# Moving the weight splits of a two-layer FFN kernel's first stage from ScalarE to GpSimd, and reordering VectorE's routing block

## The chip, the cores and the metric

One core of one Trainium2 chip runs the kernel. The metric is the device time of one execution, in microseconds. The engines are TensorE (PE in the rows; PEld is its weight load), VectorE (DVE), ScalarE (ACT), GpSimd (POOL) and SyncE (SP), whose queue issues nearly all the DMAs. Each engine works through its own list of instructions in order, and the engines are tied together by semaphores.

## The reference

x is 128x32x128 (batch, time, channel). Layer 0 is a mixed linear map (a base weight and eight low-rank experts, weighted by cond), then a normalisation, a quantisation of the activations by the maximum over everything, and a ternary weight. Layer 1 routes every batch row to two of eight gated MLPs (128 to 512 and back) and adds a shared one; a quantised gated MLP follows.

```python
def L0_ffn(x, weight, gamma, beta):
    xn = (x - mu) * rsqrt(var + EPS) * gamma + beta      # per row of 128 channels
    xq = round(clip(xn / scale)) * scale                 # scale: max |xn| over all / 127
    return einsum('bsi,oi->bso', xq, ternary(weight))
def mlp(x, g, u, d):
    return einsum(gelu(x @ g) * (x @ u), d)
x = x + L0_ffn(L0_cond(x, cond_8, ...))
y = sum over the row's top-2 experts of w[e] * mlp(x, skill_*[e]) + mlp(x, shared_*)
x = x + L1_ffn(y, w_gate, w_up, w_down)
```

## The kernel before

All products are made in float32r. To keep accuracy, a matrix is split into a high half, which is the matrix copied to float32r, and a low half, the matrix minus the high half; a product is then three matmuls.

**The rounds.** The first stage is a software pipeline of 12 rounds, `n` = 0 to 11, over 8 groups of 512 columns (`i`). Each engine has its own loop over n with the same stages. TensorE transposes x (`turns`), multiplies it with the low-rank matrices (`hidden`) and with the base weight (into the bank `AZ`), sums squares (into `AV`) and spreads the reciprocal deviation over the partitions. ScalarE copies the high half of x (`xTh`), makes the squares (`sq`) and the scaled product (`xnT`), and two rounds later adds beta. VectorE makes the low half (`xTl`), multiplies the hidden part (`hs`), writes variance plus epsilon (`ST`, called ST(i) below, counter `d_var`), multiplies by the reciprocal deviation (`xnT`, xnT(i) below) and takes the maximum. GpSimd raises ST to the power -0.5 (`ST<-ST,KC`, pow(i) below, counter `k_rst`). ST(i) and pow(i) stand in round i + 2; xnT(i) in round i + 3.

**What is slipped in between.** In rounds 2 to 5 VectorE also computes the routing: many operations of 8 to 480 elements on the tiles RT, KS, etC, etF, etA, tmpP and Pm. The last and longest piece stands in round 4 and is called the routing block below.

**The weight splits.** 19 weight tiles are loaded in turn into eight staging buffers `stg`: 16 expert gate and up weights, which are split into a ring of five buffers `wst` and stored to DRAM (`wscr`), and three of the shared MLP, which stay in SBUF. `SPLITS[n]` says how many are split in round n. ScalarE makes the high half (`a_whi`), GpSimd the low half (`k_wlo`). SP waits for low half n, issues its store, then the load that reuses the staging buffer, and from n = 11 on the loads of the down weights (`wdr`). The high halves of the down weights (`down_high`) are made by ScalarE, five of them in rounds 8 to 11, and three later.

**The mixed block.** After the rounds the maximum is found, x is rounded (`round_xn`), multiplied with the ternary weight and added to x, transposed again and split into `XT`, in a second pipeline over `j`; the first eight of the shared MLP's tiles run in it. ScalarE's first copy to XT waits until all 19 low halves are made, since XT lies over stg. GpSimd makes the low halves of the down weights and of the first four shared tiles in turn (`down_low`, `shared_low`), then gathers the columns of the first expert tile (`fetch`, tile `xg`). After that come the expert tiles on TensorE (`xg,Wr`).

Of the kernel before, what the change touches and what calls it, by code (L numbers as in the profile page):

```python
# [16 lines left out]
ADD, SUB, MUL = ALU.add, ALU.subtract, ALU.mult  # L17
# [32 lines left out]
def program(nc, x, cond, Wb, bb, As, Bs, fw, gamma, beta, sg, su, sd, hg, hu, hd, wg, wu, wd, out):  # L50
    ctx = ExitStack()
    with ctx:
# [137 lines left out]
        s_stg = [sem(f"s_stg{i}") for i in range(8)]  # L190
        s_wst = [sem(f"s_wst{i}") for i in range(WRING)]
        s_wr = [sem(f"s_wr{i}") for i in range(3)]
        s_wz, d_ov = sem("s_wz"), sem("d_ov")
# [15 lines left out]
        k_tab, d_tab, p_tab = sem("k_tab"), sem("d_tab"), sem("p_tab")  # L209
        k_wlo, k_rst = sem("k_wlo"), sem("k_rst")  # L210

        d_col, p_max, d_top = sem("d_col"), sem("p_max"), sem("d_top")

# [34 lines left out]
        IOTA, PART, TRI0, IDENT, TRI, CTR, HALVES, MEAN, NONE, PLACES = 3, 4, 5, 6, 7, 8, 9, 10, 11, 12  # L248
        SPLITS = (0, 2, 2, 2, 2, 2, 2, 2, 2, 3, 0, 0)
        LARGEST = {10: 0, 12: 1, 14: 2, 18: 3, 22: 4, 26: 5, 30: 6, 33: 7}  # L250

        WDS = {8: (0,), 10: (1, 2), 11: (3, 4)}

# [485 lines left out]
        def _(e):  # L739
# [65 lines left out]
            for n in range(12):  # L805
# [85 lines left out]
                if n in (5, 6, 7, 8):  # L891
                    if n == 5:
                        w.wait_ge(k_const, PART)
                        cp(bcF[:, :], bcI[:, :]).then_inc(d_place, 1)
                        w.wait_ge(d_rt, n_tmp)
                        stt(Pm[:, :], iof[:, :], S[:, 43:44], tmpP[:, :], ALU.is_equal, ADD).then_inc(d_place, 1)
                        w.wait_ge(p_route, 2)
                        n_ = step(ts(S[:, 44:45], bank[6][:, 16:17], 0.7 / 16384, None, MUL))
                    if n == 6:
                        w.wait_ge(d_rt, n_)  # L900
                        n_7 = step(tt(tsc[:, :], tpos[:, :], tneg[:, :], ADD))
                        step(tt(tpos[:, :], tpos[:, :], tneg[:, :], SUB))
                        w.wait_ge(d_rt, n_7)
                        red(S[:, 46:47], tsc[:, :], ADD).then_inc(d_parts, 1)
                    if n == 7:
                        w.wait_ge(p_route, 3)
                        cp(ordI[:, :], bank[6][0:1, 0:NSLOT]).then_inc(d_ord, 1)
                    hidden(n - 1)
                if n == 9:
# [6 lines left out]
                if 0 <= i < 8:  # L916
                    for h in "ab" if i == 7 else ("",):
                        w.wait_ge(a_beta, i + 1 + (h == "b"))
                        m = 183 if h == "b" else 184 + i
                        red(S[:, m:m + 1], xnT[:, cols(i)][:, SPAN[h]], ALU.max, True).then_inc(d_mx1, 1)  # L920
                if n == 4:
                    after(n_1, n_2, n_3)
# [43 lines left out]
                if n == 9:  # L966
                    w.wait_ge(d_rt, n_)
                    n_alpha = step(tt(S[:, 142:143], S[:, 141:142], bank[6][:, 19:20], MUL))
                i = n - 2
                if 0 <= i < 8:  # L970
                    w.wait_ge(p_var, i + 1)
                    if i >= 2:
                        w.wait_ge(k_rst, i - 1)
                    ts(ST[:, i % 2, 0:4], AV[:, 0:4], 1.0, 1e-5, MUL, ADD).then_inc(d_var, 1)
                i = n - 3
# [20 lines left out]
            w.wait_ge(d_rt, n_)  # L996
            step(e.reciprocal(S[:, 183:184], S[:, 182:183]))
            w.wait_ge(d_rt, n_alpha)
            tt(S[:, 180:181], S[:, 182:183], S[:, 142:143], MUL).then_inc(d_sc, 1)

# [302 lines left out]
        def _(e):  # L1303
# [13 lines left out]
            do(S[:, 16:24], S[:, 0:8], ACT.Exp, bias=S[:, 12:13], scale=1.0, accum_out=S[:, 13:14]).then_inc(a_exp, 1)  # L1317
            split = 0

            def down_high(k):  # L1320
                w.wait_ge(s_stg[k], 64 if k < 3 else 48)
                do(WD[:, 0, cols(k)], wdr[:, k, :]).then_inc(a_wdh, 1)

            for n in range(12):
# [22 lines left out]
                if 0 <= i < 8:  # L1347
# [6 lines left out]
                    do(xnT[:, cols(i)], AZ, ACT.Identity, scale=S[:, 8:9], bias=KC[:, 6:7]).then_inc(a_zg, 1)  # L1354
                for _ in range(SPLITS[n]):
                    b = split % 8
                    w.wait_ge(s_stg[b], 16 * (split // 8 + 1))
                    if WRING <= split < NG:
                        w.wait_ge(s_wst[split % WRING], 16 * (split // WRING))
                    hi = wst[:, split % WRING, 0, :] if split < NG else SHh[split - NG][:, :] if split < NR - 1 else SD[:, 0, :]  # L1360
                    do(hi, stg[:, b, :]).then_inc(a_whi, 1)
                    split += 1
                for k in WDS.get(n, ()):
                    down_high(k)
            do(S[:, 11:12], S[:, 13:14], ACT.Gelu_apprx_tanh)


# [17 lines left out]
            def round_xn(j):  # L1385
                w.wait_ge(d_sc, QSC)
                do(xnT[:, cols(j)], xnT[:, cols(j)], ACT.Identity, scale=S[:, 183:184], bias=RMC).then_inc(a_q, 1)
# [3 lines left out]
            for j in range(12):  # L1391
                if j < 6:
                    round_xn(j + 2)
                if 1 <= j < 9:
                    i = j - 1
                    w.wait_ge(p_x1t, i + 1)
                    w.wait_ge(k_wlo, NR)
                    do(x_half(0, i), bank[5 + i % 3]).then_inc(a_xt, 1)
                    if 3 <= i < 6:
                        down_high(2 + i)  # L1400
                n = j - 2
                if n == 0:
                    for k in range(WRING):
                        w.wait_ge(s_wst[k], stored(k))
                if 0 <= n < HK:
                    shared_gelu(n)
                if 1 <= n <= HK:
                    shared_high(n - 1)
                if 2 <= n < HK + 2 and (n - 2) % 4 == 3:
                    shared_sum(n - 2)  # L1410
# [127 lines left out]
        def _(e):  # L1538
# [29 lines left out]
            for n in range(12):  # L1568
# [16 lines left out]
                for _ in range(SPLITS[n]):  # L1585
                    hi, lo = ((wst[:, split % WRING, 0, :], wst[:, split % WRING, 1, :]) if split < NG else
                              (SHh[split - NG][:, :], SHl[split - NG][:, :]) if split < NR - 1 else (SD[:, 0, :], SD[:, 1, :]))
                    w.wait_ge(a_whi, split + 1)
                    low(lo, stg[:, split % 8, :], hi).then_inc(k_wlo, 1)
                    split += 1  # L1590
# [100 lines left out]
        def _(e):  # L1691
# [28 lines left out]
            for n in range(NR):  # L1720
# [6 lines left out]
                for k in {11: (0,), 12: (1,), 13: (2,), 14: (3,), 15: (4, 5, 6, 7)}.get(n, ()):  # L1727
                    e.dma_start(wdr[:, k, :].rearrange("p (c h) -> p c h", c=4),
                                sd[k].rearrange("(c p) h -> p c h", p=128)).then_inc(s_stg[k], 16)
                if n == 9:  # L1730
# [72 lines left out]
```

## Time and profile before

| | |
|---|---|
| time, median of 3 | 400.63 us (400.24 to 400.95) |
| span of the profiled execution, first to last instruction | 398.5 us |
| TensorE busy | 346.2 us (87%) |
| VectorE busy | 330.8 us (83%) |
| ScalarE busy | 263.0 us (66%) |
| GpSimd busy | 223.4 us (56%) |

The profiled execution is known by its span; the 2.1 us between the span and the median lie before the first and behind the last instruction. The span falls into the rounds (0 to about 58 us), the mixed block (to 89.13 us), the expert tiles (to about 220 us), the rest of the shared MLP (to about 285 us) and the quantised MLP.

### The profile page before, as it was taken

Reading aid. Unit: us, or ns where it says so; the run is one execution under the profiler, and the core shown is the slowest. Engines: PE = TensorE matmul, PEld = TensorE weight load, DVE = VectorE, ACT = ScalarE, POOL = GpSimd, SP = SyncE. Lnnn points to the kernel's source line nnn. Section 1 sums busy time; section 2 is a strip of 40 time slices with the busy share of each in tenths; the row PEclk is TensorE's granted clock in tenths of the full one; section 3 lists DMA queues with packets and bytes.
Section 4 is the critical chain, followed back from the end, with each engine's and each line's share of the span. In section 5 each row is a group of like instructions: output and inputs, shape, how many; then the busy total and the mean of one; then the engine's idle time right before and its main releaser. Section 6 shows DMA issues by size and latency. Waiting matters only on the chain.

```text
span 398.5 us, 6226 instructions
## 1 busy us (share of the span) xinstructions
PE 346.2 (87%) x1754; PEld 285.0 (72%) x1754; DVE 330.8 (83%) x700; ACT 263.0 (66%) x339; POOL 223.4 (56%) x400
## 2 busy tenths in 40 slices
PE   8979967999999999999999989999999971005997
PEld 7657744768898989989898977777677650003897
DVE  4588558975999999999999989765689899979894
ACT  3655687866576565666656544555467899999650
POOL 2656885897466473847465023222195568992462
PEclk9998999999999999999999999999999996555999
DMA  6998993955353443535332005100000000000022
GB/s 173 341 398 301 326 314 118 315 161 212 112 202 111 151 168 117 201 106 187 132 127 84 3 2 160 51 2 0 1 2 0 1 0 1 0 0 2 0 108 105
DMA packets 19850, 47.77 MB, mean 120 GB/s; under 512 B 2787, under 2 KB 8934, under 8 KB 17254
## 3 DMA queue, kind: packets, MB, share of 16 engines
q1 hardware_dynamic: 18342, 47.16, 33.8%
q10 hardware_dynamic: 1472, 0.20, 0.3%
q8 instruction: 14, 0.23, 0.2%
q14 instruction: 22, 0.18, 0.1%
HBM read 33.10 MB, written 12.58 MB: 115 GB/s over the span
## 4 chain that ended last, share of the span: by engine, by line
PE 59%; DVE 15%; POOL 8%; issue 6%; DMA 6%; ACT 5%; ACTq 0%; DVEq 0%; SPq 0%; POOLq 0%
PE ps L378 57%; DVE S L755 3%; DMA wscr<-wst 2%; POOL XCh L1542 2%; POOL wst L1545 2%; DMA wdr<-n_L_cond_skill_down_dram 2%; DVE O_i L752 1%; PE ps L375 1%; DMA bsr<-in_L_cond_Bs_dram 1%; DVE G L746 1%; ACT U L1307 1%; POOL C_i L1542 1%; ACT ps L1307 1%; DVE Hl L746 1%; DVE HbS L746 1%
## 5 line engine op out<-in xcount | busy, mean ns | idle before, releaser
L1626 POOL CAST xg<-XT 128x64 fp32r x264 | 81.3, 356 | 52.6 <-DVE Hl L746 25.5
L378 PE MATMUL ps<-xg,Wr 128*128 128x384 f32 (+1 forms) x480 | 98.6, 354 | 0.3 <-issue 0.3
L378 PEld LDWEIGHTS ps<-xg,Wr 128*128 128x128 f32 x480 | 85.8, 188 | 7.5 <-issue 0.6
L1307 ACT ACTIVATE Hh<-HbS 128x512 fp32r<-128x512 f32 (+2 forms) x72 | 56.5, 785 | 46.2 <-DVE HbS L746 45.9
L746 DVE TENSOR_TENSOR HbS<-Gb,ps 128x512 f32<-128x512 f32 (+2 forms) x72 | 63.2, 878 | 21.7 <-PE ps L378 18.6
L1307 ACT ACTIVATE Gb<-ps 128x512 f32<-128x512 f32 (+2 forms) x72 | 54.1, 751 | 30.5 <-PE ps L378 28.7
L746 DVE TENSOR_TENSOR Hl<-HbS,Hh 128x768 fp32r<-128x768 f32 (+2 forms) x57 | 55.2, 969 | 2.3 <-ACT Hh L1307 1.8
L752 DVE SCALAR_TENSOR_TENSOR C<-ps,Wt,C 128x32 f32 x264 | 52.4, 279 | 2.9 <-PE ps L378 2.6
L378 PE MATMUL ps<-XT,SHh 128*128 128x512 f32 x128 | 45.7, 398 | 0.8 <-DVE XT L746 0.4
L1545 POOL TENSOR_TENSOR Hl<-HbS,Hh 128x512 fp32r<-128x512 f32 x15 | 19.7, 1316 | 47.0 <-ACT Hh L1307 46.9
L1307 ACT ACTIVATE ps<-G,S 128x1024 int32<-128x1024 f32 (+1 forms) x29 | 35.6, 1250 | 6.7 <-DVE O_i L752 5.7
L378 PE MATMUL ps<-Hh,WT 128*128 128x384 f32 (+1 forms) x160 | 37.3, 355 | 0.0
L378 PEld LDWEIGHTS ps<-Hh,WT 128*128 128x128 f32 x160 | 29.0, 188 | 2.1
L378 PEld LDWEIGHTS ps<-XT,SHh 128*128 128x128 f32 x128 | 24.0, 188 | 6.2 <-issue 0.7
L755 DVE TENSOR_REDUCE S<-G 128x1 f32<-128x1024 f32 (+1 forms) x26 | 28.1, 1125 | 0.2
L378 PE MATMUL ps<-XT,SHl 128*128 128x512 f32 x64 | 25.0, 391 | 0.0
L1545 POOL TENSOR_TENSOR wst<-stg,wst 128x512 fp32r<-128x512 f32 x16 | 20.6, 1310 | 7.2 <-ACT wst L1307 7.2
L378 PE MATMUL ps<-Hh,SD 128*128 128x512 f32 x64 | 21.4, 416 | 2.7 <-DVE Hl L746 2.7
L378 PE MATMUL ps<-Hl,WT 128*128 128x384 f32 (+1 forms) x80 | 23.1, 370 | 0.2 <-DVE Hl L746 0.2
L378 PE MATMUL ps<-WFd,G 128*128 128x128 f32 x192 | 22.0, 276 | 0.5 <-POOL G L1542 0.4
L378 PEld LDWEIGHTS ps<-WFd,G 128*128 128x128 f32 x192 | 21.7, 192 | 1.1 <-issue 1.1
L1542 POOL TENSOR_SCALAR G<-O_i 128x1536 f32<-128x1536 int16 (+2 forms) x12 | 12.5, 1045 | 17.6 <-DVE O_i L752 17.5
(222 smaller groups left out, 675.7 us busy)
## 6 DMA issues: line engine op xcount, KB each, us to landing
Wr<-wscr SPq DMA_DIRECT2D x20, 1024.0 KB, 4.8
wscr<-wst SPq DMA_DIRECT2D x16, 512.0 KB, 5.9
stg<-n_L_cond_skill_gate_dram SPq DMA_DIRECT2D x8, 256.0 KB, 7.6
stg<-in_L_cond_skill_up_dram SPq DMA_DIRECT2D x8, 256.0 KB, 7.9
wdr<-n_L_cond_skill_down_dram SPq DMA_DIRECT2D x8, 256.0 KB, 5.8
xscr<-X SPq DMA_DIRECT2D x8, 256.0 KB, 6.1
X<-xscr SPq DMA_DIRECT2D x8, 256.0 KB, 4.3
out_dram<-X SPq DMA_DIRECT2D x7, 256.0 KB, 2.0
```

The lines of the kernel that those rows point to most:

```text
L375: return e.transpose(o_, i_, identF[:, :])
L378: return e.matmul(o_, l, r, start=start, stop=stop, skip_group_check=True)
L746: return e.tensor_tensor(o_, a, b, op)
L752: return e.scalar_tensor_tensor(out=o_, in0=a, scalar=s, in1=b, op0=op0, op1=op1)
L755: return e.tensor_reduce(o_, i_, X, op, apply_absolute_value=absv)
L1307: return e.activation(o_, i_, func, **kw)
L1542: return e.tensor_scalar(o_, a, s1, s2, op0, op1)
L1545: return e.tensor_tensor(o_, a, hi.bitcast(F32), SUB)
L1626: last = e.tensor_copy(xg[:, i % XR, :, T * s:T * s + T].rearrange("p a t -> p a t"), XT[:, :, :, bass.ds(regs[s - a_], 1)].rearrange("p a ...
```

## The change

GpSimd makes both halves of the first 13 weights: a copy to float32r, a wait for it (`k_whi`), and the low half. ScalarE makes the high halves of the last six only, in rounds 9 to 11. The counts per round change. ScalarE makes no down-weight halves in the rounds: two follow behind the rounds, ahead of the first `round_xn`, and six stand in the mixed block. The down-weight loads get semaphores of their own. VectorE's ST is moved ahead of the routing block and of what belongs to the ternary weight, and in round 5 `hidden` goes ahead of Pm. `round_xn` waits for the reciprocal alone (`d_inv`), and the scalar product behind it is a tensor_scalar.

```diff
@@ semaphores and tables
+        s_wd = [sem(f"s_wd{i}") for i in range(E)]
-        SPLITS = (0, 2, 2, 2, 2, 2, 2, 2, 2, 3, 0, 0)
+        SPLITS = (0, 2, 2, 1, 2, 1, 2, 1, 2, 2, 2, 2)
+        NP = sum(SPLITS[:9])
-        WDS = {8: (0,), 10: (1, 2), 11: (3, 4)}
+        WDS = {1: (2,), 2: (3,), 3: (4, 5), 4: (6,), 5: (7,)}
@@ VectorE, round n
                     if n == 5:
+                        hidden(4)
+                        w.wait_ge(p_route, 2)
+                        n_ = step(ts(S[:, 44:45], bank[6][:, 16:17], 0.7 / 16384, None, MUL))
                         w.wait_ge(k_const, PART)
                         cp(bcF[:, :], bcI[:, :]).then_inc(d_place, 1)
...
-                    hidden(n - 1)
+                    if n > 5:
+                        hidden(n - 1)
...
+                i = n - 2
+                if 0 <= i < 8:
+                    w.wait_ge(p_var, i + 1)
+                    if i >= 2:
+                        w.wait_ge(k_rst, i - 1)
+                    ts(ST[:, i % 2, 0:4], AV[:, 0:4], 1.0, 1e-5, MUL, ADD).then_inc(d_var, 1)
                 if n == 4:
                     after(n_1, n_2, n_3)
...
-                i = n - 2
-                if 0 <= i < 8:
-                    w.wait_ge(p_var, i + 1)
-                    if i >= 2:
-                        w.wait_ge(k_rst, i - 1)
-                    ts(ST[:, i % 2, 0:4], AV[:, 0:4], 1.0, 1e-5, MUL, ADD).then_inc(d_var, 1)
...
-            step(e.reciprocal(S[:, 183:184], S[:, 182:183]))
+            e.reciprocal(S[:, 183:184], S[:, 182:183]).then_inc(d_inv, 1)
             w.wait_ge(d_rt, n_alpha)
-            tt(S[:, 180:181], S[:, 182:183], S[:, 142:143], MUL).then_inc(d_sc, 1)
+            ts(S[:, 180:181], S[:, 182:183], S[:, 142:143], None, MUL).then_inc(d_sc, 1)
@@ ScalarE
-            split = 0
+            split = NP
             def down_high(k):
-                w.wait_ge(s_stg[k], 64 if k < 3 else 48)
+                w.wait_ge(s_wd[k], 16)
...
-                for _ in range(SPLITS[n]):
+                for _ in range(SPLITS[n] if n >= 9 else 0):
...
-                for k in WDS.get(n, ()):
-                    down_high(k)
             do(S[:, 11:12], S[:, 13:14], ACT.Gelu_apprx_tanh)
+            for k in range(2):
+                down_high(k)
...
-                w.wait_ge(d_sc, QSC)
+                w.wait_ge(d_inv, 1)
...
-                    if 3 <= i < 6:
-                        down_high(2 + i)
+                    for k in WDS.get(i, ()):
+                        down_high(k)
@@ GpSimd
-                    w.wait_ge(a_whi, split + 1)
+                    if split < NP:
+                        w.wait_ge(s_stg[split % 8], 16 * (split // 8 + 1))
+                        if split >= WRING:
+                            w.wait_ge(s_wst[split % WRING], 16 * (split // WRING))
+                        e.tensor_copy(hi, stg[:, split % 8, :]).then_inc(k_whi, 1)
+                        w.wait_ge(k_whi, split + 1)
+                    else:
+                        w.wait_ge(a_whi, split + 1 - NP)
                     low(lo, stg[:, split % 8, :], hi).then_inc(k_wlo, 1)
```

GpSimd at the end of the rounds, before: the last two powers with two low halves between them, the three table operations (vneg, tmpP, iof), the three shared low halves, and the clearing of C that opens its part of the mixed block.

```order
L1545 TENSOR_TENSOR wst<-stg,wst 128x512 [waits a_whi] x2
L1575 TENSOR_TENSOR ST<-ST,KC 128x4 [waits p_rst,d_var]
L1542 TENSOR_SCALAR vneg<-vint 128x480 [waits d_place,k_const]
L1542 TENSOR_SCALAR tmpP<-iof,S 128x480
L1542 TENSOR_SCALAR iof<-iof,S 128x480 [waits k_tab,d_et]
L1545 TENSOR_TENSOR SHl_70<-stg,SHh_68 128x512 [waits a_whi]
L1545 TENSOR_TENSOR SHl_71<-stg,SHh_69 128x512 [waits a_whi]
L1545 TENSOR_TENSOR SD<-stg,SD 128x512 [waits a_whi]
L1600 MEMSET C 128x1088 [waits p_tab,d_tab]
```

The same place in the changed kernel:

```order
L1596 CAST wst<-stg 128x512 [waits s_wst1,s_stg3]
L1549 TENSOR_TENSOR wst<-stg,wst 128x512 [waits k_whi]
L1596 CAST wst<-stg 128x512 [waits s_wst2,s_stg4]
L1549 TENSOR_TENSOR wst<-stg,wst 128x512 [waits k_whi]
L1579 TENSOR_TENSOR ST<-ST,KC 128x4 [waits p_rst,d_var]
L1546 TENSOR_SCALAR vneg<-vint 128x480 [waits d_place,k_const]
L1546 TENSOR_SCALAR tmpP<-iof,S 128x480
L1546 TENSOR_SCALAR iof<-iof,S 128x480 [waits k_tab,d_et]
L1549 TENSOR_TENSOR wst<-stg,wst 128x512 [waits a_whi] x3
L1549 TENSOR_TENSOR SHl_70<-stg,SHh_68 128x512 [waits a_whi]
L1549 TENSOR_TENSOR SHl_71<-stg,SHh_69 128x512 [waits a_whi]
L1549 TENSOR_TENSOR SD<-stg,SD 128x512 [waits a_whi]
```

Two splits ahead of the last power are now four operations, and behind the tables stand three more low halves than before.

VectorE in round 4, before: the end of the routing block (RT to etF), then ST(2) and xnT(1).

```order
L746 TENSOR_TENSOR S<-S,RT 128x8 x2
L746 TENSOR_TENSOR etA<-etA,etF 1x10
L755 TENSOR_REDUCE S<-S 128x2
L746 TENSOR_TENSOR etA<-etA,etB 1x10
L743 COPY etF<-etA 1x6
L746 TENSOR_TENSOR etF<-etF,etA 1x10
L749 TENSOR_SCALAR ST<-ps 128x4
L746 TENSOR_TENSOR xnT<-ps,xnT 128x512
L749 TENSOR_SCALAR tmpP<-iof,S 128x480
```

The same place in the changed kernel:

```order
L748 TENSOR_TENSOR S<-S,RT 128x8 x2
L748 TENSOR_TENSOR etA<-etA,etF 1x10
L757 TENSOR_REDUCE S<-S 128x2
L748 TENSOR_TENSOR etA<-etA,etB 1x10
L745 COPY etF<-etA 1x6
L748 TENSOR_TENSOR etF<-etF,etA 1x10
L748 TENSOR_TENSOR xnT<-ps,xnT 128x512
L751 TENSOR_SCALAR tmpP<-iof,S 128x480
```

ST(2) has left this place and stands in front of the block; xnT(1) stays behind it.

ScalarE in the mixed block, changed kernel: round_xn (xnT), the copies to XT, the gelu (Gb) and the high half of the hidden tiles (Hh), with the down weights (WD) between.

```order
L1311 ACTIVATE XT<-ps 128x512 [waits p_x1t]
L1311 ACTIVATE WD<-wdr 128x512 [waits s_wd2]
L1311 ACTIVATE Gb<-ps 128x512 [waits s_wst3,s_wst4,s_wst2,p_sg,s_wst1,s_wst0]
L1311 ACTIVATE xnT<-xnT,S_54,S 128x512
L1311 ACTIVATE XT<-ps 128x512 [waits p_x1t]
L1311 ACTIVATE WD<-wdr 128x512 [waits s_wd3]
L1311 ACTIVATE Gb<-ps 128x512 [waits p_sg]
L1311 ACTIVATE Hh<-HbS 128x512 [waits d_sh]
L1311 ACTIVATE xnT<-xnT,S_54,S 128x512
L1311 ACTIVATE XT<-ps 128x512 [waits p_x1t]
L1311 ACTIVATE WD<-wdr 128x512 [waits s_wd4]
L1311 ACTIVATE WD<-wdr 128x512 [waits s_wd5]
```

Before, the first two of these WD rows were absent and one stood where two stand in the third place.

## Rows read from the trace of the kernel before

**Rows 1.** The page's busy times: us, share of the span, instructions.

```profile
PE 346.2 (87%) x1754; PEld 285.0 (72%) x1754; DVE 330.8 (83%) x700; ACT 263.0 (66%) x339; POOL 223.4 (56%) x400
```

**Rows 2.** Chain that ended last, 0 to 62 us: start, us, what.

```profile
13.40 8.16 DMA wscr<-wst
```

**Rows 3.** GpSimd's timeline: start, us, line, output and input, count, idle before.

```profile
21.43 2.51 POOL L1545 TENSOR_TENSOR wst<-stg,wst 128x512 fp32r<-128x512 f32 x2
28.17 1.01 POOL L1575 TENSOR_TENSOR ST<-ST,KC 128x4 f32<-128x4 f32 x1 [4.23 <-DVE ST L749]
29.15 2.92 POOL L1545 TENSOR_TENSOR wst<-stg,wst 128x512 fp32r<-128x512 f32 x2
...
39.55 1.01 POOL L1575 TENSOR_TENSOR ST<-ST,KC 128x4 f32<-128x4 f32 x1 [3.17 <-DVE ST L749]
...
53.17 1.01 POOL L1575 TENSOR_TENSOR ST<-ST,KC 128x4 f32<-128x4 f32 x1 [1.53 <-DVE ST L749]
...
56.90 1.96 POOL L1542 TENSOR_SCALAR iof<-iof,S 128x480 f32<-128x480 f32 x1 [0.18 <-POOL tmpP L1542]
...
61.61 1.45 POOL L1545 TENSOR_TENSOR SD<-stg,SD 128x512 fp32r<-128x512 f32 x1
...
73.61 1.29 POOL L1545 TENSOR_TENSOR Hl<-HbS,Hh 128x512 fp32r<-128x512 f32 x1
...
85.13 3.83 POOL L1626 CAST xg<-XT 128x64 fp32r x12 [0.53 <-issue]
```

**Rows 4.** ScalarE's timeline, same columns.

```profile
21.65 0.63 ACT L1307 ACTIVATE wst<-stg 128x512 fp32r<-128x512 f32 x1 [2.38 <-DMA wscr<-wst]
22.18 0.58 ACT L1307 ACTIVATE xTh<-ps 128x512 fp32r<-128x512 f32 x1
...
49.97 0.63 ACT L1307 ACTIVATE WD<-wdr 128x512 fp32r<-128x512 f32 x1 [1.82 <-DMA wdr<-n_L_cond_skill_down_dram]
...
64.75 0.60 ACT L1307 ACTIVATE XT<-ps 128x512 fp32r<-128x512 f32 x1 [1.35 <-PE ps L375]
...
72.91 0.63 ACT L1307 ACTIVATE Hh<-HbS 128x512 fp32r<-128x512 f32 x1
```

**Rows 5.** VectorE's timeline, same columns.

```profile
23.40 0.56 DVE L752 SCALAR_TENSOR_TENSOR RT<-KS,S 128x8 f32<-128x8 f32 x1
...
25.89 0.22 DVE L749 TENSOR_SCALAR RT<-RT 128x8 f32<-128x8 f32 x2
...
27.93 0.16 DVE L749 TENSOR_SCALAR ST<-ps 128x4 f32<-128x4 f32 x1
28.04 0.69 DVE L746 TENSOR_TENSOR xnT<-ps,xnT 128x512 f32<-128x512 f32 x1
...
29.85 1.08 DVE L752 SCALAR_TENSOR_TENSOR Pm<-iof,S,tmpP 128x480 f32<-128x480 f32 x1
...
59.48 0.96 DVE L746 TENSOR_TENSOR S<-S 128x1 f32<-128x1 f32 x1
```

**Rows 6.** GpSimd's groups by form: count, busy us, mean ns, idle.

```profile
L1542 POOL TENSOR_SCALAR C<-C_i 128x512 f32<-128x512 int16 x2 | 1.2, 620 | 0.3 <-POOL XCh L1542 0.3
```

**Rows 7.** The tile XCh: count, duration ns min/median/max, first and last start.

```profile
L1542 POOL TENSOR_SCALAR XCh<-C,S x8: 686/1120/1642, 288.8 to 301.3; 128x512 fp32r<-128x512 f32 x8
```

**Rows 8.** TensorE's timeline, columns as in rows 3.

```profile
20.02 0.60 PE L375 MATMUL ps<-identF,X 128*128 128x128 f32 x4
...
30.11 1.05 PE L378 MATMUL ps<-KC,sq 128*128 128x1 f32 x8 [1.36 <-ACT sq L1307]
...
89.13 4.69 PE L378 MATMUL ps<-xg,Wr 128*128 128x384 f32 x24
```

**Rows 9.** Stretches: length, PE busy (count), granted clock, DMA share, GB/s.

```profile
31.00:32.00 1.00, 1.00 (x7) 0.64 0.79 317
...
34.00:35.00 1.00, 1.00 (x4) 0.65 1.01 393
```

**Rows 10.** DMA issues: count, KB each, median us to landing.

```profile
wscr<-wst SPq DMA_DIRECT2D x16, 512.0 KB, 5.9
```

More of the change, by code:

```diff
@@ L209, in program @@
         k_tab, d_tab, p_tab = sem("k_tab"), sem("d_tab"), sem("p_tab")
-        k_wlo, k_rst = sem("k_wlo"), sem("k_rst")
-        d_col, p_max, d_top = sem("d_col"), sem("p_max"), sem("d_top")
+        k_whi, k_wlo, k_rst = sem("k_whi"), sem("k_wlo"), sem("k_rst")
+        d_col, p_max, d_top, d_inv = sem("d_col"), sem("p_max"), sem("d_top"), sem("d_inv")
         d_sc = sem("d_sc")
@@ L896, in _ @@
                         stt(Pm[:, :], iof[:, :], S[:, 43:44], tmpP[:, :], ALU.is_equal, ADD).then_inc(d_place, 1)
-                        w.wait_ge(p_route, 2)
-                        n_ = step(ts(S[:, 44:45], bank[6][:, 16:17], 0.7 / 16384, None, MUL))
                     if n == 6:
@@ L1728, in _ @@
                     e.dma_start(wdr[:, k, :].rearrange("p (c h) -> p c h", c=4),
-                                sd[k].rearrange("(c p) h -> p c h", p=128)).then_inc(s_stg[k], 16)
+                                sd[k].rearrange("(c p) h -> p c h", p=128)).then_inc(s_wd[k], 16)
                 if n == 9:
```

## The prediction

> **What bounds the kernel now.** The page's table of busy time is read first: TensorE is busy 87% of the span [rows 1]. That is an average. From the expert tiles on (89.13 us) TensorE runs almost without a gap, and nothing of the change is issued there, so a shift of that start shifts the end by as much. The change lies wholly in front of it: eight rounds of normalisation (to about 58 us) and the mixed block after them.
>
> Next the chain of waits, from 0 to 62 us [rows 2]: it goes through an 8.16 us store of split weights to DRAM, through VectorE's routing arithmetic, and later through a load of down weights. Both transfers hold ScalarE, as its timeline shows [rows 4]: 2.38 us in front of split 5, with x's next high half (xTh) queued behind it, and 1.82 us in front of the first down weight. So ScalarE's conversions do cost rounds, and the change has something to win there.
>
> The two places that decide what is won are read from GpSimd's timeline [rows 3]. The last power of the variances, pow(7), starts at 53.17, then come three table operations to 58.86, then the halves of the three shared weights to 63.06. ScalarE's first XT copy, which waits for all 19 low halves, starts at 64.75 [rows 4]. So GpSimd is off the path by 1.7 us here. The second place is the start of the experts: GpSimd's first fetch ends at 88.96 [rows 3], TensorE's first expert product starts at 89.13 [rows 8]. GpSimd has 0.17 us of slack there.
>
> **The change part by part.**
>
> *The rounds up to pow(7).* ScalarE loses 13 copies of 0.63 us and both waits. The wait in round 4 kept xTh back: it starts at 22.18, the transpose it reads ended at 20.62 [rows 4, 8], so about 1.5 us come free, and hs follows. ST(2) stood behind the routing block (25.89 to 27.93) and now stands ahead: 27.93 - 2.0 - 1.2 = about 24.7 [rows 5]. The block itself would then end near 26.8 and the product xnT(1) start there instead of at 28.04, 1.2 to 1.4 us earlier. ScalarE's next square and TensorE's next variance hang on xnT(1), so this is what the rounds gain, and I carry 1.4 through rounds 5 to 7, whose waits among the other three engines are unchanged. The second wait is gone too: without it the square of the last round follows TensorE's product, and ST(7) comes at about 50.4, some 2.5 earlier.
>
> *GpSimd's new load.* It now makes the high half first. The copy 128x512 float to float32r is in no row. One-input operations of 512 elements take 620 ns (C) and, for XCh, which writes float32r, 686 at least and 1120 in the median [rows 6, 7]. I take 0.62, since neither scale nor stride is needed; the range is 0.62 to 1.12. The low half takes 1.26 undisturbed, half of 2.51 [rows 3], and its wait for the copy 0.16, taken from the 0.18 ahead of the iof operation [rows 3]: 2.05 us a split. From pow(4), at 39.55 - 1.4 = 38.2, to pow(7) stand three powers of 1.0 and five splits: 3.0 + 5 x 2.05 = 13.3, and 0.3 of waiting for ST(6): pow(7) at 51.8. GpSimd, not ST(7) at 50.4, sets it. With a copy of 1.12 it would be 54.3.
>
> The Trainium skill (GPSIMD Engine Reference, section 3, its per-element model) gives 769 ns for 512 elements in a one-input loop. The rows of 620 and 686 speak against that; by the page's figure pow(7) would be 0.7 us later (an estimate).
>
> *The collision.* Where VectorE has an operation with two SBUF inputs while GpSimd works on a pair of SBUF tiles, it waits for GpSimd's operation to end. The RT operation of 8 elements that started at 23.40 took 0.56 us and ended at 23.96, as GpSimd's pair 21.43 + 2.51 ended (23.94); Pm took 1.08 and GpSimd's pair beside it 2.92 instead of 2.51 [rows 3, 5]. In the kernel before GpSimd stands idle from 23.94 to 28.17, waiting for the very variance that the routing block delays, so the block runs free. Now ST(2) goes first, pow(2) starts at about 24.9, and from 26.0 to 30.2 GpSimd has splits 5 and 6. The last seven operations of the block, most with two SBUF inputs, and the 480-element tmpP behind xnT(1), meet it. With one of them let through for each GpSimd operation, xnT(1) comes at about 28.8, 2.0 later than free, and pow(7) at 51.8 + 2.2 = 54.0. I take two thirds of that, since how many slip through at each boundary depends on tenths of a microsecond: pow(7) at 53.2. That is no change from 53.17. **Term one: 0** (from -3.0 to +0.8).
>
> The Trainium skill (SBUF — State Buffer, section "Who interferes with whom") says that the port pair shared by VectorE and GpSimd is locked for a whole instruction, by a VectorE instruction with two SBUF inputs too. The rows above agree. It speaks against putting the variance first.
>
> *The tail on GpSimd.* Before, three low halves followed the tables; now six do (splits 13 to 18). From pow(7): 5.69 us to the end of the tables (58.86 - 53.17), 6 x 1.37 = 8.2 for the halves (between 1.26 in the rounds and 1.40, the mean of the three from 58.86 to 63.06 [rows 3]), 0.1 to ScalarE: 14.0. So XT(0) starts at 53.2 + 14.0 = 67.2 instead of 64.75. **Term two: +2.4.** VectorE is dense from XT(0) on and TensorE after it, so nothing absorbs it. That ScalarE reaches its rounding of xnT up to 0.4 later (two down weights now stand ahead of it, and the new d_inv wait lets it go 0.9 sooner) is hidden in front of that wait, and the tt that became ts was a 0.96 us wait for GpSimd [rows 5], hidden too. Its cover is 2.4 us.
>
> *The down weights among the mixed rounds.* ScalarE makes six there instead of three, 0.52 us apart. Its idle time up to 70 us is used up by the first ones: Gb(1) comes 0.33 later, Hh(1) 0.85. GpSimd started the low half of Hh(1) at 73.61, with Hh(1) ending at 73.54 and no idle of its own up to 84.6 [rows 3, 4]. So it is 0.84 later, the fetch too, less the slack of 0.17. **Term three: +0.7** (0 if ScalarE's copies fill gaps). The down-weight loads move on SP behind stores 13 to 15; two are early, the rest land some 6 us after issue, before ScalarE asks.
>
> **Sum.** 0 + 2.4 + 0.7 = +3.1 us. The span was 398.5; the median is 400.63, 2.1 around it. 401.6 + 2.1 = 403.7. A measurement of this kernel tells about 0.2% (0.8 us) from no change.
>
> **The rivals.**
> *The rounds win more than the tail costs (faster).* The clock fell to 1.2 GHz from 31 to 35 us, after a gap of TensorE of 1.36 us that ended at 30.11 [rows 8, 9]. If the gap closes, the throttled stretch (4.75 us where the same work at full clock takes 3.1) is won, pow(4) is at 36.6 and pow(7) at 49.9 to 50.2. With no collision and no term three: 49.9 + 14.0 - 64.75 = -0.9, so 399.7. It decides from a pow(7) before 49.9. Against it: the gap in front of the fourth variance remains, since sq(3) still waits for xnT(1).
> *Gain and tail cancel (no change).* As above, with term three: 50.2 + 14.0 - 64.75 + 0.7 = +0.15, so 400.8. This is also what comes if the change does little.
> *Full collision, and the clock falls again (slower still).* pow(7) at 54.0 gives +3.9; TensorE then idles some 3 us before XT(0), and if its clock drops as at 31 us, 1.7 more: +5.6, so 406.2. The stores fit here: the last is issued 9.9 us behind pow(7), and the median landing is 5.9 [rows 10], which is some 0.7 ahead of the first Gb that waits for it; 2 us more of landing would cost 1.3.
>
> **How the numbers follow.** Forecast 0.46 (own range 401.6 to 405.2), no-change case 0.20, faster case 0.14, the worse case 0.20. Slower by over 0.2%: 0.46 + 0.20 = 0.66; within: 0.20; faster: 0.14. The range 400.0 to 406.3 leaves out about 0.1 on either side.
>
> **What would show it.** Right: GpSimd without idle from pow(4) to pow(7) and again to XT(0), XT(0) ending a wait on GpSimd's SD at 66 to 68 us, routing operations of 0.3 to 1.3 us beside GpSimd's splits, the first expert product at 91.5 to 93. Wrong: copies well off 0.62, pow(7) before 50, routing operations of 0.15 us throughout, or ScalarE's XT(0) released by TensorE as before.

## The result, and the profile after

The changed kernel takes 404.44 us in the median of 4 runs (403.65 to 406.08), the kernel before 400.79 (4 runs) beside it. The ratio is 1.0102, with a 95% interval of 1.0070 to 1.0134: slower by 1%, 3.65 us. The profiled execution took 403.65, the lowest of the four, with a span of 401.9 against 398.5. Medians here and below are over all executions of a kernel, while ratios leave out a few slow ones: one of a_dvelow, two of b_best (588.97 and 1191.78 us) and two of the kernel before. The page of the changed kernel, busy times and the chain that ended last by engine:

```profile
PE 347.3 (86%) x1754; PEld 285.6 (71%) x1754; DVE 333.5 (83%) x700; ACT 255.9 (64%) x326; POOL 230.0 (57%) x413
PE 56%; POOL 19%; DVE 10%; issue 7%; ACT 5%; DMA 1%; POOLq 1%; DVEq 0%; ACTq 0%
```

Against [rows 1], ScalarE has 13 operations fewer and GpSimd 13 more. The chain says more: GpSimd, 8% of it before, is 19% now, and DMA fell from 6% to 1%. So the two transfers that the prediction found on the path are off it, and GpSimd's work is on it. GpSimd's timeline, the first two splits, the stretch around the third power, and the end of the stage (start, us, line, output and input, count, idle before):

```profile
10.05 0.61 POOL L1596 CAST wst<-stg 128x512 fp32r<-128x512 f32 x1 [6.29 <-DMA stg<-n_L_cond_skill_gate_dram]
10.75 1.29 POOL L1549 TENSOR_TENSOR wst<-stg,wst 128x512 fp32r<-128x512 f32 x1
...
24.18 1.02 POOL L1579 TENSOR_TENSOR ST<-ST,KC 128x4 f32<-128x4 f32 x1 [1.41 <-DVE ST L751]
25.16 0.61 POOL L1596 CAST wst<-stg 128x512 fp32r<-128x512 f32 x1
25.85 1.29 POOL L1549 TENSOR_TENSOR wst<-stg,wst 128x512 fp32r<-128x512 f32 x1
...
52.77 1.00 POOL L1579 TENSOR_TENSOR ST<-ST,KC 128x4 f32<-128x4 f32 x1
...
58.43 3.91 POOL L1549 TENSOR_TENSOR wst<-stg,wst 128x512 fp32r<-128x512 f32 x3
62.30 2.86 POOL L1549 TENSOR_TENSOR SHl<-stg,SHh 128x512 fp32r<-128x512 f32 x2
65.12 1.27 POOL L1549 TENSOR_TENSOR SD<-stg,SD 128x512 fp32r<-128x512 f32 x1
```

The copy takes 0.61 us and the low half starts 0.70 behind its start, so a split costs some 1.9. pow(2) starts at 24.18 instead of 28.17 [rows 3], yet pow(7) only 0.40 us earlier (52.77 against 53.17). Behind the tables stand six low halves, to 66.39. ScalarE's timeline, the first XT copy:

```profile
66.48 0.60 ACT L1311 ACTIVATE XT<-ps 128x512 fp32r<-128x512 f32 x1 [3.83 <-POOL SD L1549]
```

It waited 3.83 us and was released by the last low half; before, a transpose of TensorE released it [rows 4]. What became of the early variance is in VectorE's timeline:

```profile
25.25 0.53 DVE L748 TENSOR_TENSOR RT<-RT 128x8 f32<-128x8 f32 x1
25.82 1.33 DVE L748 TENSOR_TENSOR S<-S,RT 128x8 f32<-128x8 f32 x2
...
27.27 0.45 DVE L748 TENSOR_TENSOR etA<-etA,etB 1x10 f32<-1x10 f32 x1
...
27.85 0.68 DVE L748 TENSOR_TENSOR xnT<-ps,xnT 128x512 f32<-128x512 f32 x1
28.45 0.88 DVE L751 TENSOR_SCALAR tmpP<-iof,S 128x480 f32<-128x480 f32 x1
```

Two operations on eight elements take 1.33 us, from 25.82 to 27.15; GpSimd's low half beside them ran from 25.85 to 27.14. TensorE's timeline, fourth variance, first shared product, first expert product:

```profile
29.92 1.11 PE L380 MATMUL ps<-KC,sq 128*128 128x1 f32 x8 [3.24 <-ACT sq L1311]
...
67.86 0.79 PE L380 MATMUL ps<-XT,SHh 128*128 128x512 f32 x1 [2.11 <-DVE XT L748]
...
92.89 1.31 PE L380 MATMUL ps<-xg,Wr 128*128 128x384 f32 x6
```

The gap before the fourth variance is 3.24 us, against 1.36 [rows 8], and a new gap of 2.11 stands before the first shared product. Stretches around both (length, then busy time of TensorE, its weight loads, VectorE, ScalarE, GpSimd, then granted clock, DMA share, GB/s):

```profile
32.00:34.00 2.00, 2.00 (x10) 1.93 (x10) 1.24 (x6) 0.17 (x1) 1.74 (x3) 0.50 0.43 125
66.00:68.00 2.00, 0.14 (x1) 0.14 (x1) 0.89 (x2) 1.52 (x3) 0.39 (x1) 0.50 1.05 312
68.00:70.00 2.00, 2.00 (x5) 1.61 (x6) 2.00 (x5) 1.16 (x3) 1.02 (x1) 0.50 1.26 317
```

In all three the clock is 0.50, that is 1.2 GHz. Three sections add up, before and after: start to pow(7) 53.17 and 52.77 (-0.40); pow(7) to XT(0) 11.58 and 13.71 (+2.13); XT(0) to the first expert product (the mixed block) 24.38 and 26.41 (+2.03). The sum is +3.76, and the span grew by 3.4.

### The profile page after: what moved, and what is told of

Its sections match the earlier page's. It is cut to its first block, busy times and chain, and to the rows that moved or that the text cites. A ratio compares the mean times of both kernels' runs of the same rounds, so it can differ in the third digit from the quotient of the medians.

```text
span 401.9 us, 6226 instructions
## 1 busy us (share of the span) xinstructions
PE 347.3 (86%) x1754; PEld 285.6 (71%) x1754; DVE 333.5 (83%) x700; ACT 255.9 (64%) x326; POOL 230.0 (57%) x413
## 4 chain that ended last, share of the span: by engine, by line
PE 56%; POOL 19%; DVE 10%; issue 7%; ACT 5%; DMA 1%; POOLq 1%; DVEq 0%; ACTq 0%
PE ps L380 55%; POOL wst L1549 4%; DVE S L757 3%; POOL ST L1579 2%; POOL XCh L1546 2%; POOL WD L1549 2%; POOL wst L1596 2%; DVE O_i L754 1%; DMA wbr<-in_L_cond_W_base_dram 1%; DVE G L748 1%; ACT U L1311 1%; POOL C_i L1546 1%; ACT ps L1311 1%; POOL Hl L1549 1%; DVE Hl L748 1%
## 5 line engine op out<-in xcount | busy, mean ns | idle before, releaser
L380 PE MATMUL ps<-XT,SHh 128*128 128x512 f32 x128 | 46.6, 406 | 2.5 <-DVE XT L748 2.1
L380 PE MATMUL ps<-XCh,WFh 128*128 128x512 f32 x48 | 19.6, 409 | 2.4 <-ACT U L1311 2.4
```

What stands on the lines that cost most here:

```text
L380: return e.matmul(o_, l, r, start=start, stop=stop, skip_group_check=True)
```

## The experiments

They ran in three groups, each beside the kernel before on the same chip (its medians 400.19, 400.41 and 399.92). A ratio is to that kernel, with its 95% interval. "a_" starts from the changed kernel, "b_" from the one before.

**Undo the tail: a_tail3.** The splits are handed to the rounds so that, as before, three low halves follow the tables.

```diff
-        SPLITS = (0, 2, 2, 1, 2, 1, 2, 1, 2, 2, 2, 2)
+        SPLITS = (0, 2, 2, 2, 2, 2, 2, 2, 2, 3, 0, 0)
```

> The changed kernel with the old counts per round, so that GpSimd makes both halves of all 16 expert weights ahead of its last power, and only the three shared low halves stand behind its tables. Theory (the tail): GpSimd is saturated from pow(4) on, pow(7) comes later than 52.77, about 53.5 to 54.5, but the low halves end some 9.8 us behind it, so ScalarE's XT(0) is released by TensorE again, 11.6 behind pow(7), at 65.0 to 66; TensorE's clock has less idle in front of XT(0) and falls for less long or not at all. Time 0.8 to 3 us below the changed kernel. Rival (the copies on GpSimd are what costs): three more of them ahead of pow(7) make it as slow as the changed kernel or slower.

403.08 us, 1.0064 (1.0039 to 1.0089). ScalarE's timeline:

```profile
66.56 0.60 ACT L1311 ACTIVATE XT<-ps 128x512 fp32r<-128x512 f32 x1 [1.44 <-PE ps L377]
```

TensorE releases XT(0) again, 10.04 us behind pow(7) instead of 13.71. But pow(7) comes at 56.52, later than the 53.5 to 54.5 expected, so XT(0) is no earlier. The edit doesn't touch the tail alone: it also puts a second split into rounds 3, 5 and 7. pow(2) is 1.73 us later for it, pow(4) 3.31, where the clock was 0.50 from 34 to 38 us against 0.98 in the changed kernel. The mixed block takes 24.90 instead of 26.41. By the medians this distribution of the splits is about 0.4% better (1.0064 against 1.0102), 1.5 us, but the intervals overlap, so that isn't shown.

**Are the copies the burden? a_acthigh.** ScalarE makes all high halves again; GpSimd keeps its low halves, six of them behind the tables.

```diff
-        NP = sum(SPLITS[:9])
+        NP = 0
...
-                for _ in range(SPLITS[n] if n >= 9 else 0):
+                for _ in range(SPLITS[n]):
```

> The changed kernel with ScalarE making the high halves of all 19 weights again, in the new rounds; counts per round, tail and down weights stay as changed. Theory (the tail): XT(0) still ends a wait on GpSimd's SD, about 13.7 us behind pow(7), so the time stays within 1.5 us of the changed kernel, and above the kernel before by 2 us or more. Rival (the copies on GpSimd): with them gone the time falls to that of the kernel before.

405.02 us, 1.0141 (1.0098 to 1.0184).

```profile
68.67 0.60 ACT L1311 ACTIVATE XT<-ps 128x512 fp32r<-128x512 f32 x1 [3.41 <-POOL SD L1549]
```

With no copy on GpSimd, XT(0) waits for it all the same, 14.02 us behind pow(7), and pow(7) is at 54.65 instead of 52.77 in this profile. The medians can't tell the two kernels apart. So taking the copies off GpSimd won nothing; what holds XT(0) is the place of the low halves, since with three fewer behind the tables (a_tail3) it no longer waits for them.

**The down weights alone: b_wd.** The kernel before, with ScalarE's down-weight halves and their loads moved as in the change, one semaphore for each load.

```diff
-        WDS = {8: (0,), 10: (1, 2), 11: (3, 4)}
+        WDS = {1: (2,), 2: (3,), 3: (4, 5), 4: (6,), 5: (7,)}
...
+            for k in range(2):
+                down_high(k)
...
-                    if 3 <= i < 6:
-                        down_high(2 + i)
+                    for k in WDS.get(i, ()):
+                        down_high(k)
```

> The kernel before with one part of the change: the down-weight high halves leave the rounds (two ahead of the first rounding of x, six in the mixed block), with semaphores of their own. Theory: ScalarE's wait of 1.82 us in round 8 goes, pow(7) comes 1.5 to 2.5 us sooner, XT(0) with it; in the mixed block 0.7 us is lost to the three more copies where the clock stays full. Net -0.8 to -1.8 us against the kernel before. Rival (the copies in the mixed block cost the 2.0 us that it grew by): net 0 to +0.5.

400.22 us, 0.9998 (0.9974 to 1.0022): no change. In its profile (an execution of 401.77) the mixed block takes 24.91 instead of 24.38. GpSimd's timeline, the last two powers:

```profile
50.31 1.01 POOL L1576 TENSOR_TENSOR ST<-ST,KC 128x4 f32<-128x4 f32 x1 [1.17 <-DVE ST L750]
...
54.35 1.01 POOL L1576 TENSOR_TENSOR ST<-ST,KC 128x4 f32<-128x4 f32 x1 [0.57 <-DVE ST L750]
```

From pow(6) to pow(7) are 4.04 us, against 4.99 before (48.18 to 53.17): without the 1.82 us wait for a load [rows 4] that round is 0.95 shorter, about half of what was expected. From pow(0) to pow(7) it still takes 37.76 against 37.72, since 0.99 was lost before pow(4), at a mean clock of 0.72 from 26 to 36 us against 0.83. So the wait was worth 0.95 us, and the three more halves in the mixed block took 0.5 of it back.

**The variance ahead of the routing block alone: b_var.**

```diff
+                if 0 <= i < 8:
+                    w.wait_ge(p_var, i + 1)
...
+                    ts(ST[:, i % 2, 0:4], AV[:, 0:4], 1.0, 1e-5, MUL, ADD).then_inc(d_var, 1)
...
-                if 0 <= i < 8:
-                    w.wait_ge(p_var, i + 1)
...
-                    ts(ST[:, i % 2, 0:4], AV[:, 0:4], 1.0, 1e-5, MUL, ADD).then_inc(d_var, 1)
```

> The kernel before with one part of the change: variances ahead of the routing block and of the ternary weight's work. Theory: pow(2) comes about 2 us sooner and GpSimd's splits 6 and 7 run beside the routing block, whose operations then wait for it by up to a microsecond; xnT(1), which the next rounds hang on, is later or the same. Net -0.3 to +0.8 us. Rival (the variance was the wait): net -1 us or more.

401.97 us, 1.0054 (1.0026 to 1.0081): slower by itself. The profiled execution is one of the slower of its twelve, at 403.89. VectorE's and TensorE's timelines:

```profile
26.80 1.21 DVE L746 TENSOR_TENSOR RT<-RT 128x8 f32<-128x8 f32 x1
28.05 1.26 DVE L746 TENSOR_TENSOR S<-S,RT 128x8 f32<-128x8 f32 x2
...
29.70 0.69 DVE L746 TENSOR_TENSOR xnT<-ps,xnT 128x512 f32<-128x512 f32 x1
```

```profile
31.76 1.56 PE L378 MATMUL ps<-KC,sq 128*128 128x1 f32 x8 [4.51 <-ACT sq L1307]
```

Three operations on eight elements take 2.47 us. The product xnT(1) starts 1.7 us later than before, at 29.70, and TensorE's gap is 4.51.

**Undo that part alone: a_varback.** The changed kernel with the same block back behind the routing block.

> The changed kernel with the variances back behind the routing block and the ternary weight's work. Theory: the routing block runs undisturbed and xnT(1) comes no later than 27.9, but pow(2) and GpSimd's splits behind it come 2 us later, and GpSimd, with both halves to make, has to catch up; pow(7) within 1 us of 52.77. Net -0.7 to +1 us against the changed kernel. Rival (the collision is what costs): net -1.5 us or more.

401.84 us, 1.0041 (1.0013 to 1.0070), against the changed kernel's 1.0102: the intervals meet only at 1.0070. VectorE's, TensorE's and ScalarE's timelines:

```profile
25.42 0.24 DVE L748 TENSOR_TENSOR S<-S,RT 128x8 f32<-128x8 f32 x2
...
26.15 0.69 DVE L748 TENSOR_TENSOR xnT<-ps,xnT 128x512 f32<-128x512 f32 x1
```

```profile
28.23 1.05 PE L380 MATMUL ps<-KC,sq 128*128 128x1 f32 x8 [1.50 <-ACT sq L1311]
```

```profile
63.25 0.60 ACT L1311 ACTIVATE XT<-ps 128x512 fp32r<-128x512 f32 x1 [3.22 <-POOL SD L1549]
```

The pair that took 1.33 us takes 0.24; xnT(1) comes 1.70 earlier than in the changed kernel and 1.89 earlier than before, and pow(7) is at 49.55, 3.22 earlier than in the changed kernel. The clock stayed at 1.00 from 26 to 36 us. The wait for GpSimd's SD stays: from pow(7) to XT(0) are 13.70 us, as in the changed kernel.

**The clock in round 5: a_warm5.** The changed kernel with 13 extra products in the gap ahead of the fourth variance; their result is thrown away.

```diff
+                if n == 5:
+                    busy(13, bank[0][:, 0:128], identF[:, :], identF[:, :])
```

> The changed kernel with 13 products of 128x128 of the identity by itself added on TensorE in round 5, behind the hidden product, where it is idle for 3.24 us; no part of the reference's computation. The collision stays: xnT(1) at 27.9. Theory (the collision costs 1.7 us by itself and 1.1 to 1.6 more by the clock that falls behind the longer gap): the clock stays full at 30 to 36 us, pow(4) comes at about 37.3 instead of 38.84, and the time is 1 to 1.6 us below the changed kernel. Rival (the clock's fall is hidden behind VectorE's work there): no change.

402.89 us, 1.0076 (1.0053 to 1.0098). Its stretch from 26 to 36 us, then that of the changed kernel:

```profile
26.00:36.00 10.00, 9.66 (x64) 7.50 (x63) 8.56 (x27) 4.64 (x7) 6.08 (x6) 1.00 0.67 259
```

```profile
26.00:36.00 10.00, 6.76 (x30) 4.94 (x29) 8.53 (x25) 3.56 (x6) 5.88 (x6) 0.83 0.65 236
```

The fourth variance is no earlier (29.97), but what follows runs at 2.4 GHz, and pow(4) starts at 37.28 instead of 38.84: 1.56 us, about the 1.7 at which the prediction priced one fall of the clock. In the medians it is 0.26%, 1 us, inside the overlap of the intervals. In the profiles the two parts add up: 1.70 us for the late xnT(1) and 1.56 for the clock make the 3.22 by which a_varback's pow(7) was earlier. How the 0.6% between the medians divides isn't shown. Nor does the gap's length alone say whether the clock falls: it fell behind 3.24 us here and behind 1.36 in the kernel before, and not behind the 1.50 of a_varback.

**The same on the kernel before: b_warm5.** Five products at the same place.

> The kernel before with 5 such products in the same place, where it is idle for 1.36 us. Theory (the clock): no fall at 31 us, pow(4) 1 to 1.6 us sooner than 39.55, the time 1 to 1.6 us below the kernel before. Rival: no change, or the clock falls anyway.

400.69 us, 1.0012 (0.9981 to 1.0044): no gain, where one was expected. In its profile the clock held at 1.00 from 26 to 36 us and pow(4) came 0.70 earlier, at 38.85, and pow(6) 1.29, at 46.89, but pow(7), at 52.78, only 0.39. The down weight in round 8 holds ScalarE up there:

```profile
49.59 0.63 ACT L1309 ACTIVATE WD<-wdr 128x512 fp32r<-128x512 f32 x1 [2.14 <-DMA wdr<-n_L_cond_skill_down_dram]
```

**The clock ahead of the mixed block: a_warm and a_warm2.** The changed kernel with extra products between the last transposes and the first shared product, 6 in each of two tiles, and ahead of the shared product 16 (a_warm) or 7 (a_warm2).

```diff
+                    if 1 <= j < 3:
+                        busy(6, bank[1][:, 0:128], identF[:, :], identF[:, :])
...
+                if n == 0:
+                    busy(7, bank[1][:, 0:128], identF[:, :], identF[:, :])
```

> The changed kernel with 28 products of 128x128 of the identity by itself added on TensorE, 6 each ahead of the second and third product with the ternary weight and 16 ahead of the first shared product, into a bank that is overwritten; they are no part of the reference's computation. They fill its idle time from 61 to 68 us. Theory (the clock): the granted clock stays at 2.4 GHz from 64 to 72 us, the stretch from XT(0) to the first expert product shrinks from 26.4 us by 0.7 to 1.5, and the time with it. Rival (ScalarE's six down weights alone): the clock is full but the stretch stays at 26 or more.

> As a_warm, with 7 instead of 16 products ahead of the first shared product (19 in all, no part of the reference's computation), so that they end where XT(0) is there and do not hold it up: in a_warm TensorE was still at them for 1.6 us. Theory (the clock): full clock from 64 to 72 us, and the stretch from XT(0) to the first expert product falls from 26.4 to about 25, what it is in a_acthigh with the same six down weights at full clock. Time 1 to 1.5 us below the changed kernel. Rival (down weights and GpSimd alone): 26 or more.

a_warm: 404.43 us, 1.0102 (1.0068 to 1.0135). Its clock is 1.00 from 62 to 72 us, but the 16 products ran to 69.6 and held the shared product back by themselves (its mixed block takes 26.06), so this run tells nothing of the clock's price. a_warm2: 403.82, 1.0101 (1.0071 to 1.0130). Its stretch, then the changed kernel's:

```profile
62.00:72.00 10.00, 9.43 (x74) 8.16 (x73) 7.57 (x12) 5.75 (x10) 7.21 (x6) 1.00 1.07 322
```

```profile
62.00:72.00 10.00, 6.59 (x31) 4.71 (x32) 7.08 (x13) 4.25 (x7) 6.85 (x6) 0.66 1.04 315
```

In this one execution the mixed block shrinks from 26.41 to 24.90 us. Between the medians no gain shows, where 1 to 1.5 us was expected. The two ratios, each known to 0.3%, leave room for 1.5 us either way, so the run neither shows that the median pays for the clock nor rules it out. The mean granted clock over the whole span was 0.945 to 0.953 in its six executions and 0.937 to 0.945 in the changed kernel's four, so it was mostly higher in the others too. Why the time didn't follow stays open.

**Down weights ahead of XT(0): a_wdearly.** Two halves ahead of the first XT copy, in the time in which it waits anyway.

```diff
-        WDS = {1: (2,), 2: (3,), 3: (4, 5), 4: (6,), 5: (7,)}
+        WDS = {2: (4,), 3: (5,), 4: (6,), 5: (7,)}
...
+                    if i == 0:
+                        down_high(2)
+                        down_high(3)
```

> The changed kernel with down weights 2 and 3 made by ScalarE right ahead of its first XT copy, where it waits for GpSimd for 3.8 us, and one down weight in each of four later rounds. Theory (the clock and ScalarE's down weights share the 2.0 us): Hh(0) and Hh(1) come 0.5 to 1 sooner and the first expert product 0.3 to 0.9, so the time falls by as much. Rival (the clock alone): no change beyond 0.2 us.

406.07 us, 1.0136 (1.0098 to 1.0174). ScalarE's timeline:

```profile
68.00 0.63 ACT L1311 ACTIVATE WD<-wdr 128x512 fp32r<-128x512 f32 x1 [2.83 <-DMA wdr<-n_L_cond_skill_down_dram]
68.53 0.58 ACT L1311 ACTIVATE XT<-ps 128x512 fp32r<-128x512 f32 x1
```

The second half's data weren't there, and XT(0) stood behind it until 68.53, 2.05 later than in the changed kernel. SP issues this load only when GpSimd has made low half 14, one of the six in the tail (58.93 to 66.89 here), and these loads land 5.9 us after issue in the median: the tail delays them too. It traded one wait for a worse one, and leaves its own question, what the three halves cost, to the comparison below.

**Three low halves on VectorE: a_dvelow.** The shared weights' low halves go to VectorE, behind the scale of the quantisation.

```diff
+            for m in range(3):
...
+                low(lo, stg[:, (NG + m) % 8, :], hi).then_inc(d_wlo, 1)
```

> The changed kernel with the low halves of the three shared weights made by VectorE, behind the scale and ahead of the rounded x, and not by GpSimd. Theory (the tail): GpSimd's last low half ends at about 62.3 instead of 66.4, VectorE is idle when it makes the three (some 2 to 3 us with waits for GpSimd), XT(0) comes at 64 to 65.5, the clock does not fall, and the time is 1.5 to 3.5 us below the changed kernel. Rival (something else than the tail holds XT(0), such as the stores): less than 0.5 us.

404.61 us, 1.0104 (1.0064 to 1.0144): nothing won. VectorE's and GpSimd's timelines:

```profile
58.86 3.47 DVE L748 TENSOR_TENSOR SHl<-stg,SHh 128x512 fp32r<-128x512 f32 x2
62.26 1.75 DVE L748 TENSOR_TENSOR SD<-stg,SD 128x512 fp32r<-128x512 f32 x1
```

```profile
58.84 4.62 POOL L1554 TENSOR_TENSOR wst<-stg,wst 128x512 fp32r<-128x512 f32 x3
```

Both engines have operations of the same kind at the same time and take turns: three on GpSimd take 4.62 instead of 3.91, three on VectorE 5.2. XT(0) is at 66.64, now released by TensorE, whose input VectorE made late. The tail moved; it did not shrink.

**Put together: b_best.** The kernel before, with the five extra products, down weights 0 to 2 later in the rounds, 3 behind them and 4 ahead of the first XT copy, and the changed kernel's d_inv wait and its ts. High halves stay on ScalarE, and the variance stays behind the routing block.

```diff
-        WDS = {8: (0,), 10: (1, 2), 11: (3, 4)}
+        WDS = {10: (0,), 11: (1, 2)}
...
+                if n == 5:
+                    busy(5, bank[0][:, 0:128], identF[:, :], identF[:, :])
...
+            down_high(3)
...
-                w.wait_ge(d_sc, QSC)
+                w.wait_ge(d_inv, 1)
+                if j == 1:
+                    down_high(4)
```

> The kernel before with what the runs found to be of use: the 5 products of b_warm5; down weight 0 made in round 10 instead of 8, weights 1 and 2 in round 11, 3 behind the rounds and 4 ahead of the first XT copy, so that ScalarE waits for no load in round 8 and the mixed block has three as before; and the d_inv wait and the tensor_scalar of the change. GpSimd's and VectorE's order and ScalarE's high halves are those of before. Expected: 1.5 to 3 us below the kernel before, from the clock (1 to 1.6) and ScalarE's wait and rounding (0.5 to 1.5). If the wait in round 8 was covered by others, only the first.

399.34 us, 0.9965 (0.9935 to 0.9996): by the ratio 1.4 us faster than the kernel before, and the only version here that is. In its profile pow(7) is at 51.24, XT(0) at 63.32, the mixed block 24.44. From pow(0) to pow(4) it is 0.98 us shorter than the kernel before, and from pow(6) to pow(7) 0.95 (4.04 us, as in b_wd), while 0.50 is lost between pow(7) and XT(0). So the wait for the load in round 8 was not all covered by others. The result falls just short of the 1.5 to 3 us expected, and its interval almost touches 1.

**The mixed block over the profiles.** Its length beside the clock from 66 to 70 us and the number of down weights that ScalarE makes in it:

| kernel | down weights in it | clock 66 to 70 | mixed block, us |
|---|---|---|---|
| before, b_var, b_warm5, b_best | 3 | 1.00, 0.97, 1.00, 1.00 | 24.38, 24.38, 24.41, 24.44 |
| b_wd, a_tail3, a_acthigh, a_warm2 | 6 | 1.00 in all | 24.91, 24.90, 24.95, 24.90 |
| a_dvelow, a_warm5 | 6 | 0.59, 0.65 | 25.15, 25.88 |
| changed kernel, a_varback | 6 | 0.50, 0.55 | 26.41, 26.47 |

a_warm is left out, since its own products held the block up. So is a_wdearly, with four down weights in the block, a clock of 0.50 and 26.12 us. Down the first two rows the clock is nearly the same and the down weights cost 0.5 us. From the second row on, the down weights are the same and the time is longer where the clock is low, by up to 1.5 us, though not in step with it: a_dvelow at 0.59 lost 0.2, a_warm5 at 0.65 lost 1.0.

## Why the prediction was right

403.7 was predicted and 404.44 measured, slower, inside both ranges (401.6 to 405.2 and 400.0 to 406.3). The direction was right for the reasons given, a collision on VectorE and a longer tail on GpSimd, but the sum came out as close as it did because errors of opposite sign met. Step by step:

*Term one, the rounds: 0, measured -0.40 us.* The mechanism held, but that the term is near 0 is in part luck. Without the collision pow(7) was put at 51.8, and a_varback shows it at 49.55; the collision was put at 2.2 us and carried at two thirds, 1.5, and the profiles show 3.22, 1.70 of it the late xnT(1) and the rest the clock (1.56 in a_warm5). 49.55 is what the rival "faster" gave for a throttled stretch that is won (49.9). ScalarE no longer waits for the store or the load, pow(2) came at 24.18 (predicted 24.9), and the routing block then met GpSimd's splits. Worked out was that xnT(1) comes 2.0 later than free; a_varback, where it is free, shows 1.70. b_var shows that the variance ahead of the block costs 0.5% on its own, a_varback that taking it back out of the change gives 0.6%. So a part that looks as if it could only help is a cost, and the only part of the change whose cost the medians show. The claim that one operation gets through for each GpSimd operation is roughly what the rows show: waits of 0.4 at 25.25 (to 25.78, as GpSimd's copy ended at 25.77), 1.1 at 25.82, 0.3 at 27.27. Two details were off. The second gain, ST(7) some 2.5 earlier at 50.4, was mis-sized: it was 51.80 in the trace, and b_wd and b_best show that without the load's wait pow(7) follows pow(6) 0.95 us sooner. And GpSimd was said to have no idle time from pow(4) to pow(7), but waited 1.40 before pow(6) and went from work to work before pow(5) and pow(7): a split costs 1.92, not 2.05, and GpSimd, not ST(7), still set pow(7), 0.97 us behind it.

*The copy: 0.62 us taken, 0.61 measured.* The row of 620 ns that was chosen over the 1120 of XCh was the right neighbour. The Trainium skill (GPSIMD Engine Reference, section 3) has 769 ns as the best case of a tight loop over 512 elements, by which a copy would be 0.16 longer; the trace disagrees with that figure for this copy.

*Term two, the tail: +2.4, measured +2.13.* From pow(7) to XT(0) 14.0 us were worked out; the changed kernel took 13.71, a_varback 13.70, a_warm5 13.69, a_acthigh 14.02. XT(0) ends a wait on SD at 66.48, inside the 66 to 68 named. The six low halves took 8.0, not 8.2. No medians show what the tail costs: a_tail3 gives about 0.4%, less than the 2.1 us in the profile and within the overlap of the intervals, and there the low halves hold pow(7) up instead.

*Term three, the down weights: +0.7, measured +2.03 for the same stretch.* This is the step that was mis-sized, by what it left out. Its own part, three more halves, is 0.5 us by the table above. The other 1.5 us is TensorE's clock, which fell as it idled before its first shared product. The prediction had this, but in the rival of full collision (1.7 us), on the condition that TensorE idles about 3 us; it idled 1.01, 0.26, 0.26 and 2.11 between small products, and in this execution the clock fell. The first expert product, at 92.89, is still inside the 91.5 to 93 named. That the clock causes those 1.5 us is shown for the profiled executions, by a_warm2 above all; that the median of runs pays it isn't, since a_warm2's ratio is that of the changed kernel. Of the median's 3.65 us the variance's place makes about 2.4. The rest can't be divided between tail, down weights and clock by runs with intervals of 0.3%, and a version with both the variance and the tail taken out of the change was not run.

*The gap of 3.24 us and the clock in round 5.* The prediction left the throttled stretch as it was, and it was: a mean clock of 0.60 from 31 to 35 us, against 0.57 in the kernel before. The rival "faster" needed the gap to close. It grew at its front: TensorE came to it 2.1 us sooner, while the gap ended at 29.92 instead of 30.11, for the reason given there: sq(3) waits for xnT(1), and that waited for the collision. The rival's premise was too narrow, though: in a_varback a gap of 1.50 stayed and the clock did not fall.

*The rule on the shared port.* GpSimd's pow on 128 x 4, two SBUF inputs, lasted from 24.18 to 25.20, and in it VectorE's two-input operations took 0.15 us as ever; only the 512-element copies and low halves held them up. The Trainium skill (SBUF — State Buffer, section "Who interferes with whom") has the lock for whole instructions. It agrees for the low halves (1.29 against 1.33 us) and not for this pow.

## What to carry to other kernels

Before a result is made earlier in an engine's order, look at what it releases: here it released GpSimd's 1.3 us operations into a chain of twenty small VectorE operations that had run free, and the chain lost 1.7 us. Moving work from one engine to another pays only up to the point where the other one has the last word; put its queue's end, not its mean load, against the first operation that waits for all of it. And a gap of TensorE costs its length and sometimes 1.5 us more in clock, so count each new gap twice, once as certain and once as a chance.

## What the runs showed of the hardware

The low clock doesn't sit at a fixed place. In b_wd's profile it was 0.73 from 8 to 12 us and 0.85 from 12 to 16, where the kernel before, which has the same work there, showed 1.00, and pow(0) started at 16.59 instead of 15.45; in b_best's it was 0.67 from 24 to 28 and 0.59 from 52 to 56, where most others had 1.00. Nor does it follow from the gap ahead of it alone: 1.36 us was followed by a fall in the kernel before, 1.50 by none in a_varback. An edit worth 1 us can show in one profile and not between medians (a_warm2, b_warm5), so both were needed. VectorE and GpSimd with the same kind of operation on SBUF (a_dvelow) gained a third and not half: six low halves took 5.2 us side by side, and 7.96 one after the other on GpSimd alone.
